# Alternating the products of y with those of the feed-forward layer's input, one by one

## The reference

```python
xn = layernorm(x)
q, k, v = xn@Wq+bq, xn@Wk+bk, xn@Wv+bv        # 16 heads of 16
q, k = elu(q)+1, elu(k)+1
kv  = einsum('bkhd,bkhm->bhdm', k, v)
att = einsum('bqhd,bhdm->bqhm', q, kv) / max(q . sum_k k, 1e-6)
attn = att @ Wo + bo
shared = swiglu(xn @ w_in.T) @ w_out.T         # hidden width 512
h = swiglu(xn @ w1.T)                          # routed part, two of 8 experts a row
routed = sum_e (h * w_se[:, e]) @ w2[e].T
out = x + attn + shared + routed
```

## Time and profile before

| | us |
|---|---|
| median of 3 runs | 921.02 |
| the profiled execution | 922.05 |
| its span, first to last instruction | 920.2 |
| TensorE, weight loads | 815.6 (89%) |
| VectorE busy | 694.1 (75%) |
| ScalarE busy | 367.3 (40%) |
| GpSimd busy | 403.9 (44%) |
| TensorE's mean granted clock | 0.996 |

### The profile page before, as it was taken

How to read it: one execution, slowest core, us unless ns; L and a number is a source line. 1 busy time by engine, 2 the same in 40 slices (tenths; PEclk the granted TensorE clock), 3 DMA queues, 4 the chain that set the end, 5 groups by cost and what they waited for, 6 DMA issues and landing times. The chain is left out here.

```text
span 920.2 us, 22781 instructions
## 1 busy us (share of the span) xinstructions
PE 903.5 (98%) x6982; PEld 815.6 (89%) x6983; DVE 694.1 (75%) x1816; ACT 367.3 (40%) x605; POOL 403.9 (44%) x486
## 2 busy tenths in 40 slices
PE   8999999999999999999999999999999999999996
PEld 7798988889898989888898989898888999999996
DVE  6878777787868687777878696877676777777773
ACT  5654544353545445443525454453432222222220
POOL 3654342443425243424434243434242666555554
PEclk9999999999999999999999999999999999999999
DMA  6432413132322324141323223241156888888870
GB/s 216 136 116 70 125 51 120 69 103 90 93 100 93 116 69 125 46 125 69 103 80 103 91 92 126 69 125 47 59 204 144 145 143 143 148 137 135 137 128 1
DMA packets 141992, 98.63 MB, mean 107 GB/s; under 512 B 53136, under 2 KB 133008, under 8 KB 141968
## 3 DMA queue, kind: packets, MB, share of 16 engines
q1 hardware_dynamic: 103584, 62.50, 23.7%
q0 software_dynamic: 15920, 25.32, 12.5%
q10 hardware_dynamic: 22464, 10.51, 4.8%
HBM read 53.29 MB, written 46.43 MB: 108 GB/s over the span
## 5 line engine op out<-in xcount | busy, mean ns | idle before, releaser
L350 PE MATMUL bank<-wexp_hi,xnT_hi 128*128 (+1 forms) x560 | 188.1, 336 | 1.5 <-DVE xnT_lo L1149 1.1
L352 PE MATMUL bank<-wexp_hi,xnT_lo 128*128 (+1 forms) x560 | 185.7, 332 | 0.0
L351 PE MATMUL bank<-wexp_lo,xnT_hi 128*128 (+1 forms) x560 | 185.7, 332 | 0.0
L1227 POOL TENSOR_TENSOR h_lo<-gated,h_hi 128x256 fp32r<-128x256 f32 x128 | 98.7, 792 | 141.2 <-ACT h_hi L709 141.2
L350 PEld LDWEIGHTS bank<-wexp_hi,xnT_hi 128*128 128x128 f32 x560 | 106.3, 190 | 15.1 <-issue 4.6
L352 PEld LDWEIGHTS bank<-wexp_hi,xnT_lo 128*128 128x128 f32 x560 | 106.4, 190 | 10.3
L351 PEld LDWEIGHTS bank<-wexp_lo,xnT_hi 128*128 128x128 f32 x560 | 106.4, 190 | 9.5
L350 PE MATMUL bank<-xnT_hi,win_hi 128*128 128x512 f32 x256 | 102.1, 399 | 0.0
L351 PE MATMUL bank<-xnT_lo,win_hi 128*128 128x512 f32 x256 | 100.4, 392 | 0.0
L352 PE MATMUL bank<-xnT_hi,win_lo 128*128 128x512 f32 x256 | 99.6, 389 | 0.0
L1251 POOL TENSOR_TENSOR res<-res,bo_t 128x256 f32<-128x256 f32 x64 | 49.2, 801 | 112.3 <-DMA res<-x 112.3
(11 more groups left out here) (198 smaller groups left out, 2377.4 us busy)
## 6 DMA issues: line engine op xcount, KB each, us to landing
res<-x SPq DMA_DIRECT2D x16, 512.0 KB, 3.6
out<-res SPq DMA_DIRECT2D x16, 512.0 KB, 2.8
xt<-x SPq DMA_DIRECT2D x15, 512.0 KB, 3.4
xn_d<-xt SPq DMA_DIRECT2D x15, 512.0 KB, 4.9
xt<-xn_d SPq DMA_DIRECT2D x60, 128.0 KB, 2.7
xt<-h_d SPq DMA_DIRECT2D x76, 64.0 KB
xt<-h_d ACTq DMA_DIRECT2D x76, 64.0 KB
kb<-h_d SPq DMA_DIRECT2D x76, 64.0 KB
```

What stands on the lines that cost most here:

```text
L350: e.matmul(to, w_hi, m_hi_, start=first_, stop=False, skip_group_check=free)
L351: e.matmul(to, w_hi, m_lo_, start=False, stop=False, skip_group_check=free)
L352: return e.matmul(to, w_lo, m_hi_, start=False, stop=last_, skip_group_check=free)
L1227: ins = pool.tensor_tensor(h_lo[:, j, cols], gated[:, j % 2, cols], h_hi[:, j, cols].bitcast(f32), ALU.subtract)
```

## The change

Only TensorE's program changes. In the new `hidden_and_y(j, banks, pair_of_y)` each of the 12 products of `hidden(j)` is followed by one product of y. With j = 2 these are the products of h's blocks 0 and 1 for t = 0, then for t = 1; with j = 3 those of the same blocks for t = 2 and 3. So y's blocks 0 and 1, 24 products a batch, move from behind `hidden(3)` to between the products of `hidden(2)` and `hidden(3)`. The waits that they need move with them. Behind `hidden(3)` come first y's parts with m (24 products), then h's block 2 and then block 3 (12 each). The number of products and what each computes stay the same; the order of the sum in y does not.

```diff
+            def hidden_and_y(j, banks, pair_of_y):
+
+                for half in range(2):
+                    lo = half * 512 + j * P
+                    for c in range(DC):
+                        t, i = 2 * pair_of_y + half, c
+                        w = (win_hi[:, c, lo:lo + P], win_hi[:, c, lo:lo + P], win_lo[:, c, lo:lo + P])
+                        x_ = (xnT_hi[:, c, :], xnT_lo[:, c, :], xnT_hi[:, c, :])
+                        h_ = (h_hi[:, i, t * P:(t + 1) * P], h_hi[:, i, t * P:(t + 1) * P], h_lo[:, i, t * P:(t + 1) * P])
+                        o_ = (wout_hi[:, i, :], wout_lo[:, i, :], wout_hi[:, i, :])
+                        for k in range(3):
+                            mm = pe.matmul(bank[banks[half]][:, :], w[k], x_[k], start=(c == 0 and k == 0), stop=(c == DC - 1 and k == 2))
+                            if half == 1 and c == DC - 1 and k == 2:
+                                mm.then_inc(hid_done, 1)
+                            pe.matmul(y(t), h_[k], o_[k], start=(half == 0 and i == 0 and k == 0), stop=False, skip_group_check=True)
...
                 pe.wait_ge(rg_rdy, TB * b + 3)
-                hidden(2, (0, 1))
+                pe.wait_ge(rank_rd, b + 1)
+                if first_row(b):
+                    pe.wait_ge(ffn_split, HC + 1)
+                pe.wait_ge(hlo_rdy, HC * b + 2)
+                hidden_and_y(2, (0, 1), 0)
 
                 pe.wait_ge(rg_rdy, TB * (b + 1))
-                hidden(3, (3, 7))
+                pe.wait_ge(qn_rdy, DC * b + 1)
+                hidden_and_y(3, (3, 7), 1)
...
-                pe.wait_ge(qn_rdy, DC * (b + 1))
...
-                pe.wait_ge(rank_rd, b + 1)
-                if first_row(b):
-                    pe.wait_ge(ffn_split, HC + 1)
-                for js in ((0, 1), (2,)):
-                    pe.wait_ge(hlo_rdy, HC * b + js[-1] + 1)
-                    for t in range(TB):
-                        for j in js:
-                            mm3(pe, y(t), h_hi[:, j, t * P:(t + 1) * P], h_lo[:, j, t * P:(t + 1) * P],
-                                wout_hi[:, j, :], wout_lo[:, j, :], t % 2 == 0 and j == 0, False, True)
                 pe.wait_ge(mlo_rdy, b + 1)
                 pe.wait_ge(qlo_rdy, DC * (b + 1))
-                pe.wait_ge(hlo_rdy, HC * (b + 1))
                 for t in range(TB):
                     for c in range(DC):
                         mm3(pe, y(t), qn_hi[:, c, t * P:(t + 1) * P], qn_lo[:, c, t * P:(t + 1) * P],
                             m_hi[:, c, :], m_lo[:, c, :], False, False, True)
-                    mm = mm3(pe, y(t), h_hi[:, 3, t * P:(t + 1) * P], h_lo[:, 3, t * P:(t + 1) * P],
-                             wout_hi[:, 3, :], wout_lo[:, 3, :], False, True, True)
-                    if t % 2 == 1:
-                        mm.then_inc(y_done, 1)
+                for i in range(2, HC):
+                    pe.wait_ge(hlo_rdy, HC * b + i + 1)
+                    for t in range(TB):
+                        mm = mm3(pe, y(t), h_hi[:, i, t * P:(t + 1) * P], h_lo[:, i, t * P:(t + 1) * P],
+                                 wout_hi[:, i, :], wout_lo[:, i, :], False, i == HC - 1, True)
+                        if t % 2 == 1 and i == HC - 1:
+                            mm.then_inc(y_done, 1)
```

More of the change, by code:

```diff
@@ L481, in hidden, with y @@
                 mm.then_inc(hid_done, 1)
+            def y(t):
+                return bank[5 + t // 2][:, (t % 2) * D:(t % 2 + 1) * D]
+            def hidden_and_y(j, banks, pair_of_y):
[12 more added lines that the diff above has]
+                            pe.matmul(y(t), h_[k], o_[k], start=(half == 0 and i == 0 and k == 0), stop=False, skip_group_check=True)
             def routed(t, banks):
@@ L604, in batch @@
                     mm.then_inc(info_done, 1)
-                pe.wait_ge(qn_rdy, DC * (b + 1))
-                def y(t):
-                    return bank[5 + t // 2][:, (t % 2) * D:(t % 2 + 1) * D]
-                pe.wait_ge(rank_rd, b + 1)
-                if first_row(b):
-                    pe.wait_ge(ffn_split, HC + 1)
-                for js in ((0, 1), (2,)):
-                    pe.wait_ge(hlo_rdy, HC * b + js[-1] + 1)
-                    for t in range(TB):
-                        for j in js:
-                            mm3(pe, y(t), h_hi[:, j, t * P:(t + 1) * P], h_lo[:, j, t * P:(t + 1) * P],
-                                wout_hi[:, j, :], wout_lo[:, j, :], t % 2 == 0 and j == 0, False, True)
                 pe.wait_ge(mlo_rdy, b + 1)
                 pe.wait_ge(qlo_rdy, DC * (b + 1))
-                pe.wait_ge(hlo_rdy, HC * (b + 1))
                 for t in range(TB):
```

## The result

The changed kernel takes 934.71 us (median of 4 runs, 933.88 to 935.08) beside 921.05 for the kernel before on the same chip: a ratio of 1.0147, 95% interval 1.0129 to 1.0164. The forecast was 935.6. The profiled execution took 935.08 us with a span of 933.2 (before 922.05 and 920.2), and its mean granted clock is 0.995 (before 0.996).

A forecast was written before the change was run, and what follows sets the result against it. TensorE's start-to-start spacings were taken as the bound. Waits of 14 x 1.20 = 16.8 us, less 2.3 gained by alternating, plus 0.1 in the last batch, gave +14.6 us: 935.6 us from the median, range 929 to 942.

The forecast's parts named there:

- What bounds the kernel, and the slack: TensorE's start-to-start spacings set the time; the chain from `hidden(3)` to `kb_rdy` has 1.93 us of slack.
- The wait's price: TensorE waits for `kb_rdy` before v's product of t = 2: 1.07 us in each of batches 1 to 14.
- the release: From VectorE's end at `kb_rdy` to TensorE's start: 0.14 us of the wait.
- the chain's end: `kb_rdy` comes 2.76 us later against the batch's first product, 0.83 us after TensorE wants it.
- The second wait: Product behind `kvm`: 0.13 us more a batch; as a rival 0.6 us at `kvm` or routing, 942.2 us, 8 in 100.
- The alternation's gain: Alternating 512- and 256-column products on TensorE hides weight loads: 0.15 us a batch, 2.3 us in all.
- the pair's price of 340.0 ns: One 512-column and one 256-column product alternating on TensorE take 226.7 + 113.3 ns, against 346.7 before.
- alternating is worth nothing: Rival: weights or banks in TensorE's alternating stretch cost what they cost now; 937.9 us, 10 in 100.
- The sum: Whole kernel: 16.8 us of waits, less 2.3 gained, plus 0.1 in the last batch: net +14.6 us.
- The last batch: No gain there; the landing of SyncE's zero stores covers most of the lateness before the expert part: 0.1 us lost.
- The clock: Rival: TensorE's clock falls to 1.2 GHz behind the new pauses, fourteen spells costing 24 us: 959 us, 2 in 100.

The follow-up runs named there:

- half: Changed kernel, but only `hidden(2)` alternates; `hidden(3)` runs alone, with y's blocks 0 and 1 for t = 2, 3 behind it: 922.25 us, ratio 0.9999.
- b_delay15: Kernel before, TensorE untouched, with two idle reductions (1024 and 384 columns, 1.7 us) on VectorE between gate and transposes: 922.25 us, ratio 1.0000.
- b_delay28: Kernel before, TensorE untouched, with three idle reductions (1024, 1024, 512 columns, 2.9 us) on VectorE between gate and transposes: 935.65 us, ratio 1.0141.
- grouped: Changed kernel without alternation: y's products stand together around the hidden ones, the same products staying behind the last of `hidden(3)`: 934.56 us, ratio 1.0141.
- narrow: Changed kernel, with the 24 alternating products of y computing only 128 of their 256 columns: 931.07 us, ratio 1.0100.
- b_y128: Kernel before, with all 72 products of y in place computing only 128 of their 256 columns: 914.23 us, ratio 0.9906.
- b_tr_first: Kernel before, with both transposes of the next batch's x ahead of `gate(b, 3, 7)` on VectorE: 927.3 us, ratio 1.0047.

## Why the prediction was right

- **What bounds the kernel, and the slack.** Right. `kb_rdy` was to move to T+4.47 and came at T+4.40; the statistics were to start near T+0.7 and started at T+0.59. The threshold is confirmed by half and b_delay15 on its one side and b_delay28 on the other.
- **The wait's price.** Put at 0.83 + 0.14 + 0.10 = 1.07 us. The changed kernel's row L350 behind the normaliser, which the forecast took from 456.36 (T+18.54), starts at 465.62, T+19.42: 0.88 us late, and this holds everything up to there. The terms mis-sized are the release, 450.65 - 450.60 = 0.05 us where the earlier trace rows had 0.14, and the chain's end, 0.07 early.
- **The second wait**, put at 0.13 us (VectorE at T+19.63 against TensorE at T+19.61). It didn't come: the instruction there (L1044) ends at 464.89 + 0.40, T+19.09. The chain does run 1.3 us late at relu (T+4.91, forecast T+4.95), but VectorE had made up 0.5 us of it at L1044 (T+19.09, before T+18.26). Its short instructions of the routing now run ahead of GpSimd's work on res:

```profile
446.29 0.70 DVE L914 TENSOR_TENSOR gsum<-ex 128x4 f32<-128x4 f32 x1
```

```profile
456.00 0.16 DVE L928 TENSOR_TENSOR gsum<-ex 128x4 f32<-128x4 f32 x1
```

This is the same small instruction before (first fence, while GpSimd's adds on res run from 445.94 for 3.13 us) and after (second, ahead of the adds, which begin at 456.84). The mean of the 16 is 532 ns before and 192 ns after. The Trainium skill says in "SBUF — State Buffer", section "Who interferes with whom", that a VectorE instruction with two inputs in SBUF contends with a GpSimd instruction that reads SBUF; the trace agrees. It isn't all gain: from the reciprocal's start to the end of the kvm instruction VectorE takes 465.29 - 457.63 = 7.66 us, before 456.08 - 449.81 = 6.27, where GpSimd's adds (456.84, for 2.82 us) now fall. I had named this as the unknown of the term and left it out of its value.
- **The alternation's gain**, put at 0.15 us a batch, 2.3 us in all: wrong. The step that failed is the pair's price of 340.0 ns; it is 347.1 in the trace. Before, the same products took (429.19 - 423.71) + 24 x 0.12 = 8.36 us, 348 a pair. I took the 0.11 us from the first product of y to the second as the time of a 256-column product whose load is hidden. But only the load for the 256-column product lies under the 512-column one; the load for the next 512-column product lies under the 256 columns, and there the spacing is 120 ns again (347.1 - 226.7 = 120.4). grouped, with none alternating, takes (660.78 - 57.03)/14 = 43.1 us a batch, the same as the changed kernel. The earlier trace rows held a warning: the loads there start 0.12 us apart (429.19, 429.31), while the products' rows start 0.11 apart. The rows of narrow suggest how the 0.11 arose, since a product's row can start before its weights are there; that this happens with 256 columns too isn't shown. Of the rivals, "alternating is worth nothing" was the true one in this term. The page "TensorE: Matmul & The Clock Gate" of the Trainium skill, which I cited against the gain, came to the right result. Its reason, a load of 106.7 ns under 256 columns of 109 ns (both estimates from its formula and its 262 cycles), doesn't account for the 120.0 ns measured; its section "Back-to-back issue gap" gives the 262 cycles for isolated products, with no budget for the loads.
- **The sum.** For each of batches 1 to 14 I had 1.20 - 0.15 = +1.05 us, and it was 43.12 - 42.27 = +0.85. Waits taken 0.3 too dear and a gain of 0.15 that doesn't exist partly cancelled; 1.2 us outside these batches, 0.8 of it the first one's course, made the total look closer than the terms are. The last batch, put at 0.1, gave 0.6. So the mechanism and the size of the wait were foreseen, and that the total came within 1 us of 935.6 is partly luck.
- **The clock** stayed: 1.00 in the stretch from 450 to 452 us, which holds a pause. The 14 pauses are idle times of 0.9 us at most. The pause of 2.2 us ahead of the expert part did no harm either: 1.00 from 707.20 to 712 us.

## What to carry to other kernels

Moving work from behind a step to ahead of it shortens the time in which everything hanging on that step is hidden. Before such a move, take the last instruction of the step and follow its consumers through every engine and transfer to where the moved engine waits for them next; the loss is about lateness minus slack (b_delay28: 2.9 - 1.93 = 1.0 us, measured 0.92 a batch), nothing below the threshold, and more than one chain can end near the same place, so that cutting one link shows the next. A weight load runs under the product ahead of it, so alternating wide and narrow products changes whose load is exposed and not how many are: 934.71 us alternating, 934.56 grouped.

## What the runs showed of the hardware

- 128-column products, each with its own load of 128 by 128 weights: 111.7 ns from start to start (b_y128), and 113.3 ns as the share of one in a pair with 512 columns at 226.7 (narrow). 256-column products: 120.0 ns, although neither the 111.7, if that is the load, nor the columns at the wide products' rate (113.3, an estimate from 226.7/2) take that long. What adds the 7 to 8 ns where both are nearly equal stays open.
- The start of one row of TensorE is no measure of a product's cost: a 512-column product starts 0.06 us behind a 128-column one and lasts 0.44 us instead of 0.39, which I read as a row that starts ahead of its weights. Only sums over a stretch give a spacing.
- The same low of block 3 on GpSimd took 1.45 us, and 1.89 us in b_tr_first, where it ran beside VectorE's `t_low` (L890) from 436.10 to 437.51; in the earlier trace rows the two overlap by 0.14 us only (432.75 to 432.89).
